# A fused attention and expert layer: the last step's tail with gate weights in the up phase and the last quarter in two parts

## The reference, cut to what matters

```python
scores = xt @ gate_w
ew, ei = jax.lax.top_k(scores, K)                 # K = 2 of E = 8
ew = jax.nn.softmax(ew, axis=-1)
wE = jnp.sum(ew[None, :, :] * mask, axis=-1)      # mask: which expert was picked
h = jax.nn.gelu(jnp.einsum('td,edf->etf', xt, w1) + b1[:, None, :], approximate=False)
o = jnp.einsum('etf,efd->etd', h, w2) + b2[:, None, :]
y = _layernorm(xt[None, :, :] + o, ln_g[:, None, :], ln_b[:, None, :])
out = jnp.einsum('et,etd->td', wE, y)
x = x + gb * out                                  # gb: the gate of the modulation
```

## Time and profile before

| what | us |
|---|---|
| three timed runs, median | 245.47 |
| lowest, highest | 245.43, 246.61 |
| the profiled execution, its own time | 245.09 |
| its span in the trace | 243.3 |

### The profile page before, as it was taken

One profiled execution on the slowest core, in us unless ns is written; L12 is line 12 of the kernel. 1 busy time (PEld: TensorE's weight loads), 2 busy tenths in 40 slices (PEclk: granted clock), 3 DMA queues, 4 the chain that ended last, 5 costly groups with the idle time before them and its releaser, 6 DMA issues.

```text
span 243.3 us, 7802 instructions
## 1 busy us (share of the span) xinstructions
PE 226.8 (93%) x3069; PEld 198.3 (81%) x3069; DVE 179.3 (74%) x570; ACT 155.5 (64%) x419; POOL 136.1 (56%) x254
## 2 busy tenths in 40 slices
PE   7878899999999999999999999999999999889950
PEld 3555599889988899889988999889988998679950
DVE  2898778776988499777978598759968694663275
ACT  2358439844993869664984599385975498337830
POOL 8166755366814772467625771577336752476175
PEclk9999999999999999999999999999999999999995
DMA  6950000000000000000000000000000000000000
GB/s 188 355 231 3 1 3 3 1 3 4 12 14 3 3 0 22 7 0 4 22 3 3 3 1 24 5 0 3 22 5 0 3 23 4 3 0 6 19 0 23
DMA packets 5652, 6.23 MB, mean 26 GB/s; under 512 B 336, under 2 KB 5104, under 8 KB 5360
## 3 DMA queue, kind: packets, MB, share of 16 engines
q1 hardware_dynamic: 5616, 5.74, 7.4%
HBM read 4.68 MB, written 1.05 MB: 24 GB/s over the span
## 4 chain that ended last, share of the span: by engine, by line
PE 72%; DVE 19%; POOL 5%; issue 2%; ACT 1%; POOLq 0%; ACTq 0%; DVEq 0%
PE z L1020 16%; PE score L991 6%; PE score L982 5%; DVE q_st L595 5%; PE turns L876 5%; PE turns L877 5%; PE turns L878 5%; DVE ypart L665 3%; PE score L1002 3%; PE score L1067 2%; PE z L1042 2%; PE z L1043 2%; PE z L1044 2%; PE turns L922 2%; PE turns L1088 2%
## 5 line engine op out<-in xcount | busy, mean ns | idle before, releaser
L1020 PE MATMUL z<-w,hid 128*128 128x128 f32 x480 | 61.6, 276 | 0.0
L1020 PEld LDWEIGHTS z<-w,hid 128*128 128x128 f32 x480 | 58.8, 191 | 3.1 <-issue 1.0
L489 ACT ACTIVATE hid<-turns,pack_ffn 128x256 f32<-128x256 f32 x96 | 38.6, 518 | 27.2 <-PE turns L878 27.2
L328 POOL TENSOR_TENSOR ypart<-ypart 128x256 f32<-128x256 f32 (+1 forms) x60 | 36.1, 601 | 16.0 <-DVE ypart L665 13.0
L314 POOL TENSOR_SCALAR zvar<-zss 128x4 f32<-128x4 f32 x32 | 8.2, 256 | 60.2 <-DVE zss L651 52.2
L665 DVE SCALAR_TENSOR_TENSOR ypart<-z,zcoef,ln_gG 128x128 f32<-128x128 f32 x120 | 34.1, 340 | 1.8 <-POOL zcoef L319 1.7
L315 POOL TENSOR_TENSOR zrstd<-zvar,mhalf 128x4 f32<-128x4 f32 x32 | 32.2, 1008 | 2.7
L876 PE MATMUL turns<-h_hi,w_hi 128*128 128x256 f32 x96 | 27.8, 290 | 0.2 <-DVE h_lo L733 0.2
L878 PE MATMUL turns<-h_hi,w_lo 128*128 128x256 f32 x96 | 27.0, 281 | 0.0
L877 PE MATMUL turns<-h_lo,w_hi 128*128 128x256 f32 x96 | 27.0, 281 | 0.0
L442 ACT ACTIVATE v_bd<-turns 64x512 f32<-64x512 f32 x16 | 10.1, 632 | 20.6 <-PE turns L938 20.5
(11 more groups left out here) (157 smaller groups left out, 506.0 us busy)
## 6 DMA issues: line engine op xcount, KB each, us to landing
w<-in_w SPq DMA_DIRECT2D x2, 1024.0 KB, 6.8
out_x<-yout SPq DMA_DIRECT2D x8, 128.0 KB, 1.8
x_tokens<-in_x SPq DMA_DIRECT2D x1, 896.0 KB, 6.6
ln_g<-in_ln_g SPq DMA_DIRECT2D x1, 512.0 KB
pack_mod<-in_pack_mod SPq DMA_DIRECT2D x1, 385.0 KB, 3.1
pack_proj<-in_pack_proj SPq DMA_DIRECT2D x1, 193.0 KB, 4.2
pack_att<-in_pack_att SPq DMA_DIRECT2D x1, 130.5 KB, 4.1
x_tokens<-in_x SPq DMA_DIRECT2D x1, 128.0 KB, 3.0
```

Of the source, the lines that this page charges most:

```text
L328: cf.link(g.tensor_tensor(ypart[:, tt, at:at + n, :], ypart[:, tt, at:at + n, :], ypart[:, tt, at + n:at + 2 * n, :], ALU.add))
L489: last = a.activation(hid[:, e, c, :], up_bank(i, e)[:, c * STEP:(c + 1) * STEP], ACT.Gelu, bias=b1[:, e, c:c + 1])
L1020: last = mm(z_bank(f, q)[:, e * D:(e + 1) * D], hid[:, ee, c, tt * P:(tt + 1) * P], w2[:, ee * CH + c, :], start=False, stop=e == HALF - 1 ...
```

## The change

Only the last step and its tail change; the instructions of every earlier step are the same, in the same order.

- **Gate weights.** The softmax of two is written with tanh: weights (1 - t)/2 and (1 + t)/2 with t = tanh(gdif/2). ScalarE does Tanh (`last_tanh`) behind Gelu of expert 4 in place of Exp behind all Gelus, and VectorE its `weights` in the up phase.
- **TensorE's order.** `turn_weights` goes ahead of quarter 2, `ln_b_sum` between the halves of quarter 2.
- **Last quarter in two parts.** Quarter 3 becomes two parts of two experts (`last_quarter`), in S[3] and S[0], each with its own squares, coefficients (128x2) and products.
- **Sums.** VectorE adds up experts 0 to 3 of both tiles as soon as they are there (`last_half_sum`) and adds them to x (`last_half_out`), likewise experts 4 and 5 of tile 1. GpSimd keeps experts 4 to 7 of tile 0 and its output (`last_first_tile`).

The diff, without declarations of semaphores and with empty lines dropped:

```diff
--- before.py
+++ after.py
@@ -196,6 +196,12 @@
         def up_bank(i, e):
             return (U[1], U[0], S[0] if i == STEPS - 1 else zB[0])[e % 3]
+        LAST = STEPS - 1
+        def last_bank(part):
+            return S[0] if part else S[3]
         def here(n):
@@ -319,6 +325,26 @@
                 g.tensor_tensor(zcoef[:, b, :], zrstd[:, b, :], wexp[:, tt, half * HALF:(half + 1) * HALF],
                                 ALU.mult).then_inc(coef_s, 1)
+            def last_coefficients(part):
+                cols = slice(2 * part, 2 * part + 2)
+                pool.wait_ge(ss_act, 2 * LAST + 4 + part)
+                cf.link(g.tensor_scalar(zvar[:, 1, cols], zss[:, 1, cols], 1.0 / D, FFN_EPS, ALU.mult, ALU.add))
+                cf.link(g.tensor_tensor(zrstd[:, 1, cols], zvar[:, 1, cols], mhalf[:, 0:2], ALU.pow))
+                pool.wait_ge(u_done, 4 * LAST + 2)
+                g.tensor_tensor(zcoef[:, 1, cols], zrstd[:, 1, cols], wexp[:, 1, HALF + 2 * part:HALF + 2 * part + 2],
+                                ALU.mult).then_inc(coef_s, 1)
+            def last_first_tile():
+                pool.wait_ge(u_done, 4 * LAST + 3)
+                for n in (2, 1):
+                    cf.link(g.tensor_tensor(ypart[:, 0, HALF:HALF + n, :], ypart[:, 0, HALF:HALF + n, :],
+                                            ypart[:, 0, HALF + n:HALF + 2 * n, :], ALU.add))
+                pool.wait_ge(half_sum, 1)
+                pool.wait_ge(stored, 16 * LAST)
+                g.tensor_tensor(yout[:, 0, :], ypart[:, 0, HALF, :], X[:, TILES * LAST, :], ALU.add).then_inc(y_last, 1)
             def add_experts(f, q):
                 half, tt = q // 2, q % 2
@@ -397,14 +421,15 @@
                     pool.wait_ge(h2_s, 1)
                     gated_ln(0)
                     gated_ln(1)
-                if ffn:
+                if ffn and att:
                     coefficients(f, 3)
                 if ffn and att:
                     add_experts(f, 2)
                     add_experts(f, 3)
                 if i == STEPS:
-                    add_experts(f, 0)
-                    add_experts(f, 2)
+                    last_coefficients(0)
+                    last_coefficients(1)
+                    last_first_tile()
             steps(front, body)
@@ -466,6 +491,21 @@
                 act.wait_ge(gdif_s, f + 1)
                 a.activation(gexp[:, :], gdif[:, :], ACT.Exp).then_inc(gexp_s, 1)
+            def last_tanh():
+                act.wait_ge(gdif_s, STEPS)
+                a.activation(gexp[:, :], gdif[:, :], ACT.Tanh, scale=0.5).then_inc(gexp_s, 1)
+            def last_squares(part):
+                act.wait_ge(z_done, 4 * LAST + 4 + part)
+                act.wait_ge(coef_s, 4 * LAST + 2)
+                for e in range(2):
+                    at = 2 * part + e
+                    last = a.activation(zsq[:, 1, at * D:(at + 1) * D], last_bank(part)[:, e * D:(e + 1) * D], ACT.Square,
+                                        accum_out=zss[:, 1, at:at + 1])
+                last.then_inc(ss_act, 1)
             def square_sum(f, q):
                 act.wait_ge(z_done, 4 * f + q + 1)
@@ -504,11 +544,11 @@
             def body(i, att, ffn, nxt):
                 n, f = i + 1, i - 1
                 if i == STEPS:
-                    exp_weight(f)
                     square_sum(f, 0)
                     square_sum(f, 1)
                     square_sum(f, 2)
-                    square_sum(f, 3)
+                    last_squares(0)
+                    last_squares(1)
                 if att:
                     exp(i, 0)
                 if ffn and att:
@@ -545,6 +585,9 @@
                     gelu(i, 2)
                     gelu(i, 3)
                     gelu(i, 4)
+                if i == STEPS - 1:
+                    last_tanh()
+                if att:
                     gelu(i, 5)
                     gelu(i, 6)
                     gelu(i, 7)
@@ -616,9 +659,13 @@
             def weights(f):
                 dve.wait_ge(gexp_s, f + 1)
-                cf.link(v.tensor_scalar(gden[:, :], gexp[:, :], 1.0, None, ALU.add))
-                cf.link(v.reciprocal(gw[:, :, 0], gden[:, :]))
-                cf.link(v.tensor_tensor(gw[:, :, 1], gexp[:, :], gw[:, :, 0], ALU.mult))
+                if f == LAST:
+                    v.tensor_scalar(gw[:, :, 0], gexp[:, :], -0.5, 0.5, ALU.mult, ALU.add)
+                    cf.link(v.tensor_scalar(gw[:, :, 1], gexp[:, :], 0.5, 0.5, ALU.mult, ALU.add))
+                else:
+                    cf.link(v.tensor_scalar(gden[:, :], gexp[:, :], 1.0, None, ALU.add))
+                    cf.link(v.reciprocal(gw[:, :, 0], gden[:, :]))
+                    cf.link(v.tensor_tensor(gw[:, :, 1], gexp[:, :], gw[:, :, 0], ALU.mult))
                 for tt in range(TILES):
                     for j in range(2):
                         last = v.tensor_scalar(wsel[:, tt, j, :], iota[:, :], gidf[:, tt, j:j + 1],
@@ -667,19 +714,36 @@
                 if part != 0:
                     last.then_inc(u_done, 1)
-            def add_experts(f, q):
-                half, tt = q // 2, q % 2
-                at = half * HALF
-                dve.wait_ge(u_done, 4 * f + q + 1)
+            def last_half_sum(tt):
+                dve.wait_ge(u_done, 4 * LAST + tt + 1)
                 for n in (2, 1):
-                    cf.link(v.tensor_tensor(ypart[:, tt, at:at + n, :], ypart[:, tt, at:at + n, :],
-                                            ypart[:, tt, at + n:at + 2 * n, :], ALU.add))
-                if half == 1:
-                    cf.link(v.tensor_tensor(ypart[:, tt, 0, :], ypart[:, tt, 0, :], ypart[:, tt, at, :], ALU.add))
-                    dve.wait_ge(stored, 16 * f)
-                    v.tensor_tensor(yout[:, tt, :], ypart[:, tt, 0, :], X[:, TILES * f + tt, :],
-                                    ALU.add).then_inc(y_s, 1)
+                    cf.link(v.tensor_tensor(ypart[:, tt, 0:n, :], ypart[:, tt, 0:n, :], ypart[:, tt, n:2 * n, :], ALU.add))
+            def last_half_out():
+                dve.wait_ge(lnb_out, STEPS)
+                xs = X[:, TILES * LAST:TILES * STEPS, :]
+                v.tensor_tensor(xs, xs, ypart[:, :, 0, :], ALU.add).then_inc(half_sum, 1)
+            def last_part(part):
+                at = HALF + 2 * part
+                dve.wait_ge(coef_s, 4 * LAST + 4 + part)
+                for e in range(2):
+                    last = v.scalar_tensor_tensor(ypart[:, 1, at + e, :], last_bank(part)[:, e * D:(e + 1) * D],
+                                                  zcoef[:, 1, 2 * part + e:2 * part + e + 1], ln_gG[:, LAST // PER_BATCH, at + e, :],
+                                                  ALU.mult, ALU.mult)
+                cf.link(last)
+                cf.link(v.tensor_tensor(ypart[:, 1, at, :], ypart[:, 1, at, :], ypart[:, 1, at + 1, :], ALU.add))
+                xs = X[:, TILES * LAST + 1, :]
+                if part == 0:
+                    dve.wait_ge(half_sum, 1)
+                    v.tensor_tensor(xs, xs, ypart[:, 1, at, :], ALU.add).then_inc(part_sum, 1)
+                else:
+                    dve.wait_ge(part_sum, 1)
+                    dve.wait_ge(stored, 16 * LAST)
+                    v.tensor_tensor(yout[:, 1, :], xs, ypart[:, 1, at, :], ALU.add).then_inc(y_s, 1)
             def take_gate(i):
@@ -854,16 +918,19 @@
                 if nxt:
                     for s in range(GROUPS):
                         shift(n, s)
+                if i == STEPS - 1:
+                    weights(i)
                 if i == STEPS:
-                    weights(f)
                     weights_T(f)
                     scale(f, 0)
+                    last_half_sum(0)
                     scale(f, 1)
+                    last_half_sum(1)
                     add_ln_b(f)
+                    last_half_out()
                     scale(f, 2)
-                    add_experts(f, 1)
-                    scale(f, 3)
-                    add_experts(f, 3)
+                    last_part(0)
+                    last_part(1)
             steps(front, body)
@@ -1044,6 +1111,21 @@
                 mm(by_e, ones_r[:, :], b2_rows[:, half * HALF:(half + 1) * HALF, :], start=False, stop=False,
                    skip_group_check=True)
+            def last_quarter(part):
+                pe.wait_ge(gelu_s, 8 * STEPS)
+                pe.wait_ge(p_out, 4 * STEPS)
+                tok, bank, at = slice(P, 2 * P), last_bank(part), HALF + 2 * part
+                by_e = bank[:, 0:2 * D].rearrange("p (e d) -> p e d", d=D)
+                mm(by_e, h2_hi[:, LAST % 2, tok], bc(center_r[:, :], 1, 2), start=True, stop=False, skip_group_check=True)
+                mm(by_e, h2_lo[:, LAST % 2, tok], bc(center_r[:, :], 1, 2), start=False, stop=False, skip_group_check=True)
+                mm(by_e, ones_r[:, :], b2_rows[:, at:at + 2, :], start=False, stop=False, skip_group_check=True)
+                for e in range(2):
```

(16 more changed lines are left out.)

## The result

The changed kernel takes 245.36 us (median of 22 runs), the kernel before 246.63 beside it: ratio 0.9948, 95% interval 0.9933 to 0.9964. The forecast was -1.26 us and 244.2.

What follows compares the result with a forecast made beforehand. Bound: the 6.7 us chain behind TensorE's last product. Moved products +0.68, coefficients 0.67 later in all, sums -2.12, collisions +0.19: -1.26, so 245.09 becomes 243.83; with the profiled run 0.38 below the median, 244.2 us; range 243.4 to 245.4.

Steps and rivals of the forecast that it cites:

- TensorE +0.68: Transpose (0.14) ahead of quarter 2 and ln_b product (0.54) inside it make quarter 2 end 0.68 us later, at 232.32.
- Quarter 2's end plus 1.24: GpSimd's coefficients for quarter 2 start 1.24 us after TensorE ends that quarter at 232.32, so at 233.56.
- No wait at the transpose: TensorE does not wait at the moved transpose before quarter 2: `wexp` ready by about 224.9, 4 us ahead of need.
- Sets of GpSimd: GpSimd's last coefficients: quarter 2's set takes 1.65 us, narrow sets repeat every 1.35, and sums start at 237.82.
- Sums -2.12: GpSimd's sums behind the last coefficients take 1.74 us in place of 3.86, a gain of 2.12.
- collisions +0.19: GpSimd's and VectorE's last sums delay each other, moving the end from 239.56 to 239.75.
- the certain collision: At the end, VectorE's first last sum falls into GpSimd's second; the only collision taken as certain.
- VectorE level with GpSimd: In the tail VectorE is just free as part 1's coefficients come at 237.83, and starts its products at 237.93.
- Rival 1: VectorE becomes the end, its sums held up by GpSimd, ending near 240.4: only -0.6 us, 244.9; chance 0.20.
- rival 2: Tanh not in the loaded table: two 1.28 us loads between Gelus 4 and 5; about -0.8 us, 244.7; chance 0.04.
- The rule of the port: GpSimd excludes VectorE's two-SBUF-input instructions; part 0's VectorE sum would wait to about 237.6, end near 239.9, not 239.75.
- The span: Sign to look for in the changed kernel's profile: a span near 242.0 us.

Runs made afterwards that it cites:

- e4: Changed kernel with only the ln_b product moved behind quarter 2; last step's gate product to last sum's end 22.09 us, ratio to the kernel before 0.9945.
- e8: Kernel before with only the early sums of experts 0 to 3 on VectorE; last step's gate product to last sum's end 22.92 us, ratio to before 0.9989.
- e2: Changed kernel with the last quarter whole again; last step's gate product to last sum's end 22.52 us, ratio to the kernel before 0.9962.
- e5: Changed kernel with Exp, its table load and old weights behind all Gelus; last step's gate product to last sum's end 24.08 us, ratio to before 1.0025.

## Why the prediction was right

In size and in its steps it held, with two small errors that cancelled; the absolute time was inside the range by luck (last point). Times of after are given as those of before.

- **TensorE +0.68.** Quarter 2's end plus 1.24 was to be 233.56; its set starts at 235.28 - 1.71 = 233.57. No wait at the transpose, `wexp` at 226.62 - 1.71 = 224.9 as forecast.
- **Sets of GpSimd.** A narrow set repeats every 238.41 - 237.08 = 1.33 (forecast 1.35). Quarter 2's took 1.80, not 1.65: its first instruction began inside a VectorE sum (235.10 on) and took 0.30. I had put no collision there. The sums start at 237.93, forecast 237.82.
- **Sums -2.12, collisions +0.19.** From first sum to end 1.85 (forecast 1.74 and up to 0.19). The second sum took 0.52 for 0.47, VectorE's output 0.42 for 0.29; its sum that I had called the certain collision took a clean 0.29. The end is 239.78, forecast 239.75: an error of 0.11 in one place made up for 0.08 in another.
- **VectorE level with GpSimd.** Part 1's products start at 239.71 - 1.71 = 238.0 (237.93). Rival 1 didn't come, nor did rival 2: Tanh ran at 224.56 between two Gelus, without a load.
- **The rule of the port.** VectorE's sum at 239.00 lies wholly inside the power from 238.69 to 239.39 and took 0.29, as one alone does, so a power that has begun did not hold VectorE off. The other way round GpSimd does lose time, but less than a whole wait: in e4 VectorE's sum ended at 236.53, and the product that had begun inside it ended at 236.60, not 0.20 behind it. The Trainium skill (SBUF — State Buffer, "SBUF: two separate sides"), which the prediction set beside its rows, has whichever begins first keep the port pair for the whole instruction while the other waits. The trace agrees with that in neither direction in full: by it the sum at 239.00 would have waited until 239.39, and the end was to be 239.9, not 239.78.
- **The price of the absolute time.** 244.2 was for runs like the three shown; the median of 22 is 1.2 higher for both kernels, because two of those three lay on the lower level. With 245.36 the forecast range, up to 245.4, was met by 0.04, and that was luck: nothing in the prediction allowed for the two levels. The span, forecast near 242.0, is 243.8 in this profile of the upper level.

By e8, e2 and the changed kernel the tail goes 23.50, 22.92 (early sums), 22.52 (weights and order), 22.27 (split). No run parts the early weights from TensorE's order in the step to 22.52, and the parts don't simply add up: the sums alone give 0.58, and without them everything else costs 0.84 (24.34). The early sums are what gains, and the rest is what lets them.

## What to carry to other kernels

Where a chain of small instructions ends a program, count what stands behind the last value that arrives, and move all of it that doesn't depend on that value ahead, then pay attention to which engine has room there: the early weights are worth 0 alone and 1.8 us once the order leans on them. A sum on one engine can delay the short instructions of the critical engine next to it (0.42 us in e4), so the place of non-critical sums matters too. Compare profiles from a mark behind the start-up, not from zero.

## What the runs showed of the hardware

The two levels are TensorE's first real products. Timeline before, and then after, from the start:

```profile
4.94 1.02 PE L897 MATMUL score<-silu,pack_mod 128*128 128x2 f32 x8 [0.60 <-DVE silu L742]
5.83 1.14 PE L902 MATMUL z<-pack_mod,silu 128*128 128x128 f32 x8
```

```profile
4.94 1.84 PE L964 MATMUL score<-silu,pack_mod 128*128 128x2 f32 x8 [0.60 <-DVE silu L806]
6.65 2.05 PE L969 MATMUL z<-pack_mod,silu 128*128 128x128 f32 x8
```

The same sixteen products take 2.0 or 3.8 us, nearly double, behind seven idle products and 0.60 us of rest. Of all fourteen profiles, the six on the lower level of time had 0.95 to 1.28 in the first row and the eight on the upper 1.83 or 1.84. The granted clock of this window reads 1.00 in both, so that row does not show a slower clock. The durations do. In e2's profile the reading fell to 0.50 a little later, and three idle products took 1.49 us at that reading; in e5's, on the upper level, the same three took the same 1.49 while it read 1.00, and in before's 0.81. Each time the row and, for the first two, the window that it fills, whose third number from the end is the reading. E2, then e5, then before:

```profile
8.03 1.49 PE L957 MATMUL z<-idle 128*128 128x512 bf16 x3
...
8.03:9.52 1.49, 1.49 (x5) 0.80 (x4) 1.46 (x3) 0.56 (x1) 0.00 (x0) 0.50 0.81 100
```

```profile
8.91 1.49 PE L945 MATMUL z<-idle 128*128 128x512 bf16 x3
...
8.91:10.40 1.49, 1.49 (x5) 0.80 (x4) 1.46 (x5) 0.56 (x1) 0.00 (x0) 1.00 0.95 354
```

```profile
7.82 0.81 PE L883 MATMUL z<-idle 128*128 128x512 bf16 x3
```

So on the upper level TensorE ran these idle products at the lower of its two clocks, 1.2 GHz, though the reading is 1.00; why it reads so stays open. They stand right behind the sixteen products, and that those ran at the lower clock too follows from their nearly doubled time.

The delay goes on through VectorE, which waits for these products before it makes the gates. Before, and then after:

```profile
7.34 0.15 DVE L747 TENSOR_SCALAR modT<-score 128x4 f32<-128x4 f32 x1
```

```profile
8.74 0.16 DVE L811 TENSOR_SCALAR modT<-score 128x4 f32<-128x4 f32 x1 [1.30 <-PE z L969]
```

TensorE's first attention scores start at 13.09 and 14.50, which is 1.41 of the 1.71 between the two marks; nearly all of the rest is there by the first step's gate product (32.86 and 34.52). In e2 the lower clock came only behind these products, VectorE was not held up (7.34), and the run stayed on the lower level.
